# Setup in one unrolled pipeline, routings turned through TensorE, and new operand layouts in a two-layer macaron network

## The chip, the cores and the metric

The kernel runs on one core of one Trainium2 chip. The metric is the time of one execution on the device in microseconds (us). The engines that matter here are TensorE (PE, with its weight loads as PEld), VectorE (DVE), ScalarE (ACT), GpSimd (POOL) and SyncE (SP), which issues the DMAs.

## The reference

The input x is 2 sequences of 512 tokens with 512 features each. Two layers are computed on it, and every sublayer sees a layer norm (`ln`) of x:

```
x = x + 0.5 * ffn0(ln(x));  x = x + attn0(ln(x));  x = x + 0.5 * ffn0(ln(x))
x = x + 0.5 * ffn1(ln(x));  x = x + attn1(ln(x));  x = x + 0.5 * ffn1(ln(x))

ffn0: xn = ln(x) * gamma + beta; sig = sign(xn)            # 64 tiles of 8 features, 8 clusters of 8 tiles
      tile = argmax of sig @ tile_sigs.T in the cluster with the largest sig @ cluster_sigs.T
      x_slice = the 8 features of that tile; mn, mx = its min, max over all tokens of the tile
      u = (x_slice - mn) / (mx - mn); spline by bases and slopes at u, added to the 8 features
attn0: q, k, v with biases, rotary; kp, qp = random features (sin, cos) of the unit vectors
      kv = einsum('bhsf,bhsd->bsfd', kp, v); out = einsum('bhsf,bsfd->bhsd', qp, kv) @ Wo.T + bo
      # the sum runs over the heads of one token, so tokens are independent of each other
attn1: causal differential attention, two softmaxes per head pair, o = o1 - lam * o2, rms norm, Wo
ffn1: x = fwht(x * SU_ug); up, gate = x @ W_up.T * Wscale, x @ W_gate.T * Wscale; silu(gate) * up
      x = fwht(x * SU_dp) @ W_down.T * Wscale_dp
```

The second of the two min and max tables depends on x after attn0, so ffn0 is routed twice.

## The kernel before, in words

Tokens lie on the 128 partitions. The 2,048 rows that the kernel holds are 16 token tiles of 128 (`NT`), in 4 chunks of 512 (`NCH`, `TPC` = 4 tiles each). Weights and the large activations are kept as pairs of fp16 numbers, a high part and the rest of it (names end in `_hi` and `_lo`): ACT writes the high part from PSUM and DVE the low part. Each engine has its own hand-written program; counting semaphores (`gate`) order them, and loops over chunks are hardware loops (`Fori`). The stages, by time:

1. **Setup** (`setup_sync` L480, `setup_pool` L544, `setup_tensor` L570, `setup_scalar` L629, `setup_vector` L686). PE turns three groups of layer-0 weights (L566). Then a loop of 4 iterations follows, each with two groups of W_up and W_gate: a group of 4 tiles is scaled by row on DVE (L720), turned on PE (L566), split into high and low parts by ACT (L653) and DVE (L726), multiplied by a Hadamard matrix on PE (L597, 32 matmuls of 512 columns) and split again (ACT L659, DVE L735). Each iteration also holds the first routing of one chunk: layer norm statistics (`token_stats_vector` L337: DVE L343 to L362, ACT L371 to L376), gamma and beta on POOL (L539, L541), the sign on ACT (L384) and everything else on DVE (`routing_choice` L403 and `routing_ends` L427: products and sums over 128x2048 elements). POOL mixes one of four row blocks of W_down in each iteration (L556, L558). A stage behind the loop turns, splits and multiplies W_down (PE L614, L624, L625; DVE L763, L771) and stores it to HBM.
2. **b loop** (`b_tensor` L1031 and its siblings): layer-0 attention of a chunk, with the second routing of the chunk before (`last`) and the spline and norm of the next one (`next`) inside. Rotary and features take the projections in 6 steps `z`. SP spreads the features with 36 DMAs (L1191). The attention proper takes 32 groups of 16 tokens in 16 pairs `y`: PE makes the scores of a pair (L1082, 2 matmuls of 256 columns), DVE masks them (L1260), and PE multiplies by the values (L1093, 16 matmuls of 64 columns on four column tiles).
3. **First ffn1** (L1012 products with the turned weights).
4. **c loop** (`c_tensor` L1529 and its siblings): differential attention. A step `t` takes two heads and one block of 128 keys. Its exponentials come from ACT (L1681), DVE casts them to fp16 (L1788), and the low parts are taken on DVE for head 0 (L1790) and on POOL for head 1 (L1738). PE then multiplies by the values (L1616 to L1626).
5. **Second ffn1.**

The low parts in the c loop are ordered by these lines:

```
# PE, c_tensor
gate(pe, s["c_p_lo0"], nth(i, 1, STEPS, t + 1), s["gates"])
gate(pe, s["c_p_lo1"], nth(i, 1, STEPS, t + 1), s["gates"])
# ACT, c_scalar, ahead of the exponentials of step t
if t >= 2:
    gate(e, s["c_p_lo0"], nth(i, 1, STEPS, t - 1), s["gates"])
    gate(e, s["c_p_lo1"], nth(i, 1, STEPS, t - 1), s["gates"])
```

## Time and profile before

| | us |
|---|---|
| median of 3 runs | 2706.0 (2699.02 to 2713.09) |
| the profiled execution | 2700.26 |
| its span, first to last instruction | 2697.7 |
| PE busy | 2077.6 (77%) |
| DVE busy | 1280.5 (47%) |
| ACT busy | 720.1 (27%) |
| POOL busy | 390.0 (14%) |

The profile is of one execution. Its span is 2.6 us shorter than its time on the device. The shares are averages over stages with different limits, so they say little about a change that touches three of the five stages; the table by stage further down does. A matmul group is busy from its first start to its last modelled end, so a busy PE can still be slow. The granted clock of TensorE (PEclk) has two levels here, 1.0 for 2.4 GHz and 0.5 for 1.2 GHz; a mean between them is a mixture in time.

### The profile page before, as it was taken

The page shows a single profiled execution, that of the slowest core. Times are in us where ns is not written, and L with a number is a line of the kernel's source. Part 1 is how long each engine was busy: PE and PEld are TensorE (multiplying, and loading weights), DVE is VectorE, ACT ScalarE, POOL GpSimd, SP SyncE. Part 2 cuts the span into 40 slices and gives each one's busy share as a digit, 9 for nine tenths or more (in the row PEclk, how much of TensorE's full clock was granted, in tenths as well). Part 3 has the DMA queues.
Part 4 walks back from the last instruction along what each step waited for, and adds up shares of the span by engine and source line. Part 5 has one row for each costly group of instructions (what it writes and reads, how often), then busy time and mean ns, then how long its engine had stood idle before and what let it go on. Part 6 is the DMA issues. An engine that isn't in the chain of part 4 may idle for free.

```text
span 2697.7 us, 33465 instructions
## 1 busy us (share of the span) xinstructions
PE 2077.6 (77%) x11495; PEld 935.6 (35%) x11495; DVE 1280.5 (47%) x2219; ACT 720.1 (27%) x1102; POOL 390.0 (14%) x268
## 2 busy tenths in 40 slices
PE   4343386756567619999999888787879789999998
PEld 2121232213122204444444333333334334444443
DVE  3887746555656474242412167464756622121221
ACT  2332222131221312221212135243342522121210
POOL 0666010200102000000000024132332400000000
PEclk8676675757658559999999988988979899999999
DMA  7000311010000110000000000000000010000000
GB/s 257 31 31 0 69 21 31 16 35 16 18 17 16 36 63 1 1 0 0 0 32 0 32 1 2 2 1 2 1 1 1 1 63 1 16 0 16 0 16 16
DMA packets 74133, 58.09 MB, mean 22 GB/s; under 512 B 49185, under 2 KB 60705, under 8 KB 72993
## 3 DMA queue, kind: packets, MB, share of 16 engines
q1 hardware_dynamic: 74016, 56.57, 7.3%
q8 instruction: 69, 1.13, 0.2%
q14 instruction: 48, 0.39, 0.0%
HBM read 36.63 MB, written 10.49 MB: 17 GB/s over the span
## 4 chain that ended last, share of the span: by engine, by line
PE 58%; DVE 22%; issue 7%; ACT 5%; SPq 2%; POOL 2%; DMA 1%; DVEq 1%; ACTq 0%; POOLq 0%
PE ps L1012 46%; DVE arena L1788 2%; PE ps L1082 2%; SPq L1191 2%; PE ps L1093 1%; DVE arena L435 1%; DVE arena L720 1%; DVE arena L431 1%; PE ps L1635 1%; PE ps L1597 1%; PE ps L799 1%; POOL arena L1743 1%; PE ps L1550 1%; DVE arena L343 1%; DVE arena L411 1%
## 5 line engine op out<-in xcount | busy, mean ns | idle before, releaser
L1012 PE MATMUL ps<-arena 128*128 128x512 f16 (+1 forms) x6048 | 1344.4, 383 | 60.9 <-DVE arena L1810 16.2
L1012 PEld LDWEIGHTS ps<-arena 128*128 128x128 f16 x6048 | 593.0, 99 | 787.9 <-issue 112.5
L1363 DVE SCALAR_TENSOR_TENSOR arena<-ps,arena 128x512 f32<-128x512 f32 x128 | 88.5, 692 | 441.4 <-PE ps L1012 433.9
L1337 ACT ACTIVATE arena<-ps 128x512 f32<-128x512 f32 x128 | 76.6, 598 | 529.4 <-PE ps L1012 522.0
L597 PE MATMUL ps<-arena 128*128 128x512 f16 x256 | 72.6, 453 | 127.9 <-DVE arena L726 127.9
L1392 DVE SCALAR_TENSOR_TENSOR arena<-ps,arena 128x512 f32 (+1 forms) x32 | 22.1, 691 | 307.3 <-PE ps L1012 307.3
L1738 POOL TENSOR_TENSOR arena<-arena 128x512 f16<-128x512 f32 (+3 forms) x128 | 132.9, 1038 | 223.5 <-DVE arena L1788 223.5
L1732 POOL TENSOR_TENSOR arena<-arena 128x512 f16<-128x512 f32 x32 | 37.0, 1157 | 859.8 <-ACT arena L1660 859.8
L1759 DVE TENSOR_REDUCE arena<-ps 128x2 f32<-128x256 f32 (+3 forms) x128 | 98.7, 818 | 62.8 <-PE ps L1550 60.7
L1788 DVE CAST arena<-arena 128x1024 f16<-128x1024 f32 (+3 forms) x128 | 93.5, 730 | 72.9 <-PE ps L1626 43.0
L1681 ACT ACTIVATE arena<-ps 128x1024 f32<-128x1024 f32 (+3 forms) x128 | 89.5, 701 | 91.8 <-POOL arena L1738 41.7
L1082 PE MATMUL ps<-arena 96*128 96x256 f16 x128 | 64.8, 600 | 55.8 <-DMA arena<-arena 33.7
L1170 POOL TENSOR_TENSOR arena<-arena 128x512 f32<-128x512 f32 x24 | 32.3, 1347 | 438.3 <-ACT arena L1126 438.3
L1367 DVE TENSOR_TENSOR arena<-arena 128x512 f16<-128x512 f32 x128 | 87.2, 682 | 2.0 <-ACT arena L1341 1.8
L597 PEld LDWEIGHTS ps<-arena 128*128 128x128 f16 x256 | 28.0, 112 | 170.5 <-issue 151.2
L1341 ACT ACTIVATE arena<-arena 128x512 f16<-128x512 f32 x128 | 79.6, 622 | 19.9 <-DVE arena L1363 19.9
L1597 PE MATMUL ps<-arena 32*128 32x512 f16 (+3 forms) x768 | 81.5, 320 | 0.0
L1260 DVE TENSOR_TENSOR arena<-ps,arena 128x256 f32<-128x256 f32 x128 | 48.4, 420 | 65.9 <-PE ps L1082 65.1
L1790 DVE TENSOR_TENSOR arena<-arena 128x512 f16<-128x512 f32 (+3 forms) x128 | 71.8, 561 | 15.2
L1337 ACT ACT_TABLE_LOAD x12 | 15.4, 1283 | 191.2 <-PE ps L1012 191.2
L990 PE MATMUL ps<-arena 128*128 128x128 f32 x80 | 19.5, 425 | 60.4 <-ACT arena L971 42.8
L1056 PE MATMUL ps<-arena 128*24 128x512 f32 x48 | 32.9, 777 | 34.4 <-POOL arena L1174 34.2
(235 smaller groups left out, 2473.4 us busy)
## 6 DMA issues: line engine op xcount, KB each, us to landing
arena<-arena SPq DMA_DIRECT2D x144, 64.0 KB, 2.0
arena<-_attn_hidden_states_dram SPq DMA_DIRECT2D x4, 1024.0 KB, 10.5
arena<-in_L_ffn_W_up_dram SPq DMA_DIRECT2D x8, 512.0 KB, 8.3
arena<-in_L_ffn_W_down_dram SPq DMA_DIRECT2D x4, 1024.0 KB, 14.7
arena<-in_L_ffn_W_gate_dram SPq DMA_DIRECT2D x8, 512.0 KB, 4.2
...
```

The lines of the kernel that those rows point to most:

```text
L597: ins = pe.matmul(k.ps[:, 4 + kc, :], sign, part[:, jc, :], start=(n == 0), stop=(n == 7))
L1012: ins = pe.matmul(out, left[a](c), right[b](c), start=(at == 0), stop=(at == 3 * n - 1))
L1082: ins = pe.matmul(k.ps[:, 4 + y % 2, 256 * q:256 * q + 256].rearrange("p (t h) -> p t h", h=16), k.ksg[0:96, 2 * y + q, :], k.qs[0:96, :, ...
L1337: e.activation(k.silu[:, f % 2, :], k.ps[:, 2 * (f % 2), :], ACT.Silu, scale=1.0 / (W_SCALE * A_SCALE))\
L1341: e.activation(k.act_hi[:, f - 1, :], k.prod[:, (f - 1) % 2, :], ACT.Copy).then_inc(s["f_hi"], 1)
L1363: e.scalar_tensor_tensor(out=k.prod[:, f % 2, :], in0=k.ps[:, 1 + 2 * (f % 2), :], scalar=1.0 / W_SCALE, in1=k.silu[:, f % 2, :], op0=ALU. ...
L1367: e.tensor_tensor(k.act_lo[:, f - 1, :], k.prod[:, (f - 1) % 2, :], k.act_hi[:, f - 1, :], ALU.subtract)\
L1597: pe.matmul(k.ps[:, bank, queries], x[rows, 4 + b, keys], y[rows, b, queries], start=False, stop=False)
L1681: e.activation(k.p32[:, t % 2, :, queries], k.ps[:, 2 * (t % 2):2 * (t % 2) + 2, queries], ACT.Exp, scale=SCORE)\
L1738: e.tensor_tensor(k.p_lo[:, t % 2, 1, queries], k.p32[:, t % 2, 1, queries], k.p_hi[:, t % 2, 1, queries], ALU.subtract).then_inc(s["c_p_l ...
L1759: e.tensor_reduce(k.mx[:, u, 4 * b + 2 * j:4 * b + 2 * j + 2], k.ps[:, bank:bank + 2, 0:(u + 1) * P], AXX, ALU.max).then_inc(s["c_max"], 1)
L1788: e.tensor_copy(k.p_hi[:, t % 2, :, queries], k.p32[:, t % 2, :, queries]).then_inc(s["c_p_hi"], 1)
```

## The change

**Setup.** It becomes one unrolled program. The statistics of all 16 token tiles are taken once, ahead of the 4 iterations. The small vectors (scales, gamma, beta, biases) are loaded as rows into `k.rt` and turned by one PE operation; gamma and beta are no longer spread over the partitions. The row scaling of W_up and W_gate (L720) is gone, and the scale is applied in ffn1 instead, where ACT and DVE take it in place of a constant. Each iteration has three groups now: two of W_up or W_gate, and one W_down block, which had its own stage. The turned tiles have 2 PSUM banks and the multiplied ones 2, where each had 4. The stores of W_down lie between the loads of later groups on SP. The loads of two biases, `bv` and `bo`, come behind the last routing.

**Routings.** Both use PE. The normed rows are turned (L416 of the new file); ACT applies gamma and beta and takes the sign, features now on the partitions. Fp16 matmuls with a matrix of signs make 64 keys for each token (L427, L429), DVE takes the maximum and the one-hot row, PE turns that (L438) and spreads it into a mask (L449), DVE multiplies 4 blocks of 512 by it (L497), and 16 fp32 matmuls with 8 columns each cut out the slice (L459).

**Attention of the b loop.** The scores lie heads first instead of tokens first. The score matmul's moving operand is read in runs of 16 fp16 numbers where each number was 1,024 bytes from the one before. The matmul with the values now reads fp32 numbers that are 64 bytes apart where it read runs of 16. The copy that prepares the keys, the mask and the load of the values (8 DMAs for 1) follow the new layout.

**c loop.** DVE takes the low parts of both heads in one operation, and POOL's L1738 is gone.

```diff
+def route_turn_tensor(k, pe, i, n, c, banks):
+
+    s = k.s
+    if c == 0:
+        gate(pe, s["z_scaled"], i + n, s["gates"])
+    if c < 2:
+        gate(pe, s["r_picked"], nth(i, n, KC, 2), s["gates"])
+    else:
+        gate(pe, s["r_y"], nth(i, n, KC, c - 1), s["gates"])
+    for u in range(TPC):
+        ins = pe.transpose(k.ps[:, banks[c % 2], u * P:(u + 1) * P], k.y[:, u, c * P:(c + 1) * P], k.c["ident"])
+    ins.then_inc(s["r_turned"], 1)
+
+
+def route_key_tensor(k, pe, i, n, bank):
+
+    s = k.s
+    gate(pe, s["r_sign"], nth(i, n, KC, KC), s["gates"])
+    gate(pe, s["r_cut"], i + n, s["gates"])
+    for u in range(TPC):
+        out = k.ps[:, bank, u * NTILE:(u + 1) * NTILE]
+        pe.matmul(out, k.one16, k.key16, start=True, stop=False)
+        for c in range(KC):
+            ins = pe.matmul(out, k.sgt[:, c, u * P:(u + 1) * P], k.tsig[:, c, :], start=False, stop=(c == KC - 1))
+    ins.then_inc(s["r_key"], 1)
+
+
+def route_hot_tensor(k, pe, i, n, bank):
+
+    s = k.s
+    gate(pe, s["r_hot"], i + n, s["gates"])
+    for u in range(TPC):
+        ins = pe.matmul(k.ps[0:NTILE, bank, u * P:(u + 1) * P], k.onehot[:, bass.ds(i * TPC + u, 1), :].squeeze(1),
+                        k.ident16, start=True, stop=True)
+    ins.then_inc(s["r_hot_turned"], 1)
+
+
+def route_mask_tensor(k, pe, i, n, c, banks):
+
+    s = k.s
+    gate(pe, s["r_oht"], i + n, s["gates"])
+    if c >= 2:
+        gate(pe, s["r_picked"], nth(i, n, KC, 2 + c - 1), s["gates"])
+    pe.matmul(k.ps[:, banks[c % 2], :], k.expand[:, c * P:(c + 1) * P], k.hot_t, start=True, stop=True)\
+        .then_inc(s["r_mask"], 1)
+
+
+def route_slice_tensor(k, pe, i, n, bank):
+
+    s = k.s
+    gate(pe, s["r_picked"], nth(i, n, KC, 2 + KC), s["gates"])
+    for u in range(TPC):
+        for c in range(KC):
+            ins = pe.matmul(k.ps[:, bank, 256 + u * DSL:256 + (u + 1) * DSL], k.y[:, u, c * P:(c + 1) * P], k.c["lane"],
+                            start=(c == 0), stop=(c == KC - 1))
+    ins.then_inc(s["r_slice"], 1)
...
+def route_sign_scalar(k, e, i, n, c, banks):
+
+    s = k.s
+    gate(e, s["r_turned"], nth(i, n, KC, c + 1), s["gates"])
+    y = feature_block(k.y, c)
+    e.activation(y, token_columns(k.ps[:, banks[c % 2], :]), ACT.Identity, bias=k.beta[:, c:c + 1],
+                 scale=k.gamma[:, c:c + 1]).then_inc(s["r_y"], 1)
+    gate(e, s["r_y"], nth(i, n, KC, c + 1), s["gates"])
+    e.activation(token_columns(k.sgt[:, c, :]), y, ACT.Sign).then_inc(s["r_sign"], 1)
...
+    gate(e, s["r_key"], i + n, s["gates"])
+    key = k.ps[:, bank, 0:TPC * NTILE].rearrange("p (u t) -> p u t", u=TPC)
+    V.link(e.tensor_reduce(k.kmax, key, AXX, ALU.max))
+    e.tensor_tensor(k.onehot[:, bass.ds(i * TPC, TPC), :], key, bcast(k.kmax.unsqueeze(2), [P, TPC, NTILE]),
+                    ALU.is_equal).then_inc(s["r_hot"], 1)
...
+    gate(e, s["r_mask"], nth(i, n, KC, c + 1), s["gates"])
+    y = feature_block(k.y, c)
+    e.tensor_tensor(y, token_columns(k.ps[:, banks[c % 2], :]), y, ALU.mult).then_inc(s["r_picked"], 1)
...
+    e.tensor_scalar(k.off, hot, 1.0, BIG, ALU.subtract, ALU.mult)
+    gate(e, s["r_slice"], i + n, s["gates"])
+    cells = k.ps[:, bank, 256:256 + TPC * DSL].rearrange("p (u j) -> p u j", u=TPC)
+    e.tensor_reduce(k.ends[:, :, 0], cells, AXX, ALU.max)
+    V.link(e.tensor_reduce(k.ends[:, :, 1], cells, AXX, ALU.min))
+    e.tensor_copy(k.sliced[:, bass.ds(i * TPC, TPC), :], cells).then_inc(s["r_cut"], 1)
     V.link(e.tensor_scalar(k.ends[:, :, 1], k.ends[:, :, 1], -1.0, None, ALU.mult))
...
+    wide = [P, TPC, 2, NTILE]
+    V.link(e.tensor_tensor(k.cand, bcast(k.off.unsqueeze(2), wide), bcast(k.ends.unsqueeze(3), wide), ALU.add))
+    V.link(e.tensor_reduce(k.best, k.cand.rearrange("p u a t -> p a t u"), AXX, ALU.max))
+    e.tensor_tensor(k.acc, k.acc, k.best, ALU.max).then_inc(s["routed"], 1)
+    gate(e, s["routed"], i + n, s["gates"])
...
+    pe.wait_ge(s["ss_set"], 1)
+    for i in range(NCH):
+        turned(i, 0)
+        mixed(i, 0, range(KC))
+        for c in range(KC):
+            route_turn_tensor(k, pe, i, 1, c, ROUTE_BANK)
+        turned(i, 1)
+        route_key_tensor(k, pe, i, 1, KEY_BANK)
+        mixed(i, 1, range(KC))
+        route_hot_tensor(k, pe, i, 1, ROUTE_BANK[0])
+        turned(i, 2)
+        for c in range(KC):
+            route_mask_tensor(k, pe, i, 1, c, ROUTE_BANK)
+        mixed(i, 2, (0, 1))
+        route_slice_tensor(k, pe, i, 1, KEY_BANK)
+        mixed(i, 2, (2, 3))
...
-    with pe.Fori(0, UG_GROUPS // 2) as i:
-        group(i, 0)
-        group(i, 1)
...
+        if g >= 3 and g % 2:
+            store_down(g // 2 - 1)
...
+    store_down(3)
+    sp.wait_ge(s["routed"], NCH)
     sp.dma_start(k.bv, d["L0_attn_bv"].partition_broadcast(P)).then_inc(s["b_in"], 16)
...
+    first(0)
+    setup_stats_vector(k, V)
+    setup_scale_vector(k, V)
+    first(1)
+    setup_norm_vector(k, V)
+    first(2)
+    for i in range(NCH):
+        turned(i, 0)
+        mixed(i, 0, range(KC))
+        turned(i, 1)
+        route_choice_vector(k, V, i, 1, KEY_BANK)
+        mixed(i, 1, range(KC))
+        turned(i, 2)
+        for c in range(KC):
+            route_pick_vector(k, V, i, 1, c, ROUTE_BANK)
+        mixed(i, 2, (0, 1))
+        mixed(i, 2, (2, 3))
+        route_ends_vector(k, V, i, 1, KEY_BANK)
...
+        if last is not None:
+            m = 1 + NCH
+            if z == 2:
+                gate(pe, s["b_v_in"], nth(i, 1, TPC, TPC + 2), s["gates"])
+            if z in (2, 3):
+                route_turn_tensor(k, pe, last, m, 2 * z - 4, SECOND_BANK)
+                route_turn_tensor(k, pe, last, m, 2 * z - 3, SECOND_BANK)
+            if z == 4:
+                route_key_tensor(k, pe, last, m, SECOND_KEY)
+            if z == 5:
+                route_hot_tensor(k, pe, last, m, SECOND_BANK[0])
+            if z >= 6:
+                route_mask_tensor(k, pe, last, m, 2 * z - 12, SECOND_BANK)
+                route_mask_tensor(k, pe, last, m, 2 * z - 11, SECOND_BANK)
...
+        if z == 4 and last is not None:
+            route_slice_tensor(k, pe, last, 1 + NCH, SECOND_KEY)
+            gate(pe, s["r_cut"], last + 2 + NCH, s["gates"])
...
-                ins = pe.matmul(k.ps[:, 4 + y % 2, 256 * q:256 * q + 256].rearrange("p (t h) -> p t h", h=16),
-                                k.ksg[0:96, 2 * y + q, :], k.qs[0:96, :, toks].rearrange("p h t -> p t h"),
-                                start=True, stop=True)
+                ins = pe.matmul(k.ps[:, 4 + y % 2, 256 * q:256 * q + 256].rearrange("p (h t) -> p h t", h=16),
+                                k.ksg[0:96, 2 * y + q, :], k.qs[0:96, :, toks], start=True, stop=True)
...
-                                    k.sm[:, (y - 1) % 2, q].rearrange("p (a j) h -> p j a h", j=4)[:, j],
+                                    k.sm[:, (y - 1) % 2, q].rearrange("p h (a j) -> p j a h", j=4)[:, j],
...
-            routing_choice(k, V, last, 1 + NCH, "")
+            route_choice_vector(k, V, last, 1 + NCH, SECOND_KEY)
...
-        routing_ends(k, V, last, 1 + NCH, "")
+        for c in range(KC):
+            route_pick_vector(k, V, last, 1 + NCH, c, SECOND_BANK)
+        route_ends_vector(k, V, last, 1 + NCH, SECOND_KEY)
...
-            e.activation(k.silu[:, f % 2, :], k.ps[:, 2 * (f % 2), :], ACT.Silu, scale=1.0 / (W_SCALE * A_SCALE))\
+            e.activation(k.silu[:, f % 2, :], k.ps[:, 2 * (f % 2), :], ACT.Silu, scale=k.wscale[:, FB + f:FB + f + 1])\
...
-        if t < STEPS:
-            queries = slice(t % TPC * P, CH)
-            gate(e, s["c_p_hi"], nth(i, 1, STEPS, t + 1), s["gates"])
-            e.tensor_tensor(k.p_lo[:, t % 2, 1, queries], k.p32[:, t % 2, 1, queries], k.p_hi[:, t % 2, 1, queries],
-                            ALU.subtract).then_inc(s["c_p_lo1"], 1)
...
-            e.tensor_tensor(k.p_lo[:, t % 2, 0, queries], k.p32[:, t % 2, 0, queries], k.p_hi[:, t % 2, 0, queries],
-                            ALU.subtract).then_inc(s["c_p_lo0"], 1)
+            e.tensor_tensor(k.p_lo[:, t % 2, :, queries], k.p32[:, t % 2, :, queries], k.p_hi[:, t % 2, :, queries],
+                            ALU.subtract).then_inc(s["c_p_lo"], 1)
```

On DVE, in one iteration of the setup loop. The names are lines and operations, `arena` is SBUF and `ps` is PSUM. Before, from the low parts of the first group to the masked rows (L726 low parts of turned tiles, L735 of multiplied ones, L408 to L424 the choice of the tile, L431 and L435 the slice):

```order
L735 SCALAR_TENSOR_TENSOR arena<-ps,arena 128x512 x4
L726 SCALAR_TENSOR_TENSOR arena<-ps,arena 128x4x128 x4
L408 TENSOR_TENSOR arena<-arena 128x2048
L411 TENSOR_REDUCE arena<-arena 128x256
L412 TENSOR_REDUCE arena<-arena 128x32
L414 SCALAR_TENSOR_TENSOR arena<-arena 128x256
L417 SCALAR_TENSOR_TENSOR arena<-arena 128x64 x4
L422 TENSOR_REDUCE arena<-arena 128x4
L424 TENSOR_TENSOR arena<-arena 128x256
L735 SCALAR_TENSOR_TENSOR arena<-ps,arena 128x512 x4
L431 TENSOR_TENSOR arena<-arena 128x2048
L435 TENSOR_REDUCE arena<-arena 128x32
```

After, the same place (L901 low parts of turned tiles, L910 and L916 of multiplied ones, L487 and L488 the choice, L497 the masked rows, L508 to L510 the slice from PSUM):

```order
L910 SCALAR_TENSOR_TENSOR arena<-ps,arena 128x512 x4
L901 SCALAR_TENSOR_TENSOR arena<-ps,arena 128x4x128 x4
L487 TENSOR_REDUCE arena<-ps 128x4
L488 TENSOR_TENSOR arena<-ps,arena 128x256
L910 SCALAR_TENSOR_TENSOR arena<-ps,arena 128x512 x4
L901 SCALAR_TENSOR_TENSOR arena<-ps,arena 128x512 x4
L497 TENSOR_TENSOR arena<-ps,arena 128x4x128 x4
L916 SCALAR_TENSOR_TENSOR arena<-ps,arena 128x512 x4
L505 TENSOR_SCALAR arena<-arena 128x256
L508 TENSOR_REDUCE arena<-ps 128x4
L509 TENSOR_REDUCE arena<-ps 128x4
L510 COPY arena<-ps 128x32
```

The seven operations of the choice have become two, the product and the reduction over 2,048 elements have become four products of 512, and the W_down group (the second L901 and L916) stands in the iteration.

On SP, at the end of setup (L524 and L634 load the random matrix, L531 and L623 store W_down). Before:

```order
L524 DMA arena<-in_L_attn_rand_matrix_dram 32x16x1 x8
L526 DMA arena<-in_L_attn_bv_dram 128x256
L527 DMA arena<-in_L_attn_bo_dram 128x512
L531 DMA wd_hi_dram<-arena 2048x1x128
L531 DMA wd_lo_dram<-arena 2048x1x128
```

After:

```order
L634 DMA arena<-in_L_attn_rand_matrix_dram 32x16x1 x8
L623 DMA wd_hi_dram<-arena 2048x1x128
L623 DMA wd_lo_dram<-arena 2048x1x128
L638 DMA arena<-in_L_attn_bv_dram 128x256
L639 DMA arena<-in_L_attn_bo_dram 128x512
```

The two biases have moved behind the last store and the last routing. PE and DVE wait for them, as before, ahead of the first spline.

On PE, in an iteration of the b loop, between the last norm sums (L1056, L1219) and the angles of the features (L1066, L1246), where L1063 and L1243 are the six projections. Before:

```order
L1056 MATMUL ps<-arena 24x512 x2
L1063 MATMUL ps<-arena 128x512 x5
...
L1063 MATMUL ps<-arena 128x512
L1066 MATMUL ps<-arena 128x512 x6
```

After:

```order
L449 MATMUL ps<-arena 128x512 x2
L1219 MATMUL ps<-arena 24x512
...
L449 MATMUL ps<-arena 128x512 x2
L1243 MATMUL ps<-arena 128x512 x4
...
L459 MATMUL ps<-arena 128x8 x16
...
L1243 MATMUL ps<-arena 128x512
...
L1243 MATMUL ps<-arena 128x512
L1246 MATMUL ps<-arena 128x512 x6
```

The mask and the slice of the second routing now stand in front of two of the projections.

## Rows read from the trace of the kernel before

**Rows 1.** Windows, whole kernel: stretch, busy of each engine (instructions), PEclk, DMA share, GB/s.

```profile
39.00:279.00 240.00, 90.08 (x400) 45.74 (x400) 183.06 (x248) 76.44 (x108) 130.50 (x40) 0.68 0.12 42
279.00:312.00 33.00, 18.92 (x186) 17.49 (x187) 23.10 (x40) 15.65 (x29) 0.00 (x0) 0.81 0.66 130
...
1380.00:2160.00 780.00, 658.29 (x4639) 289.78 (x4637) 404.95 (x620) 270.31 (x423) 189.74 (x176) 0.91 0.01 4
2160.00:2698.00 538.00, 516.57 (x2399) 235.35 (x2397) 121.51 (x223) 103.80 (x173) 0.00 (x0) 0.99 0.04 16
```

**Rows 2.** Timeline, third setup iteration: start, length, engine, line, operation, [idle before <-releaser].

```profile
170.20 2.28 DVE L720 TENSOR_TENSOR arena<-arena 128x2048 f32<-128x2048 f32 x1
170.67 8.99 PE L597 MATMUL ps<-arena 128*128 128x512 f16 x32 [27.01 <-DVE arena L726]
...
179.50 1.91 PE L566 MATMUL ps<-arena 128*128 128x128 f32 x16
...
182.75 2.93 ACT L376 ACTIVATE arena<-arena 128x512 f32 x4 [2.92 <-DVE arena L362]
...
187.87 2.06 ACT L653 ACTIVATE arena<-ps 128x512 f16<-128x512 f32 x4
189.26 2.47 DVE L726 SCALAR_TENSOR_TENSOR arena<-ps,arena 128x512 f16<-128x512 f32 x4
...
217.93 3.83 DVE L435 TENSOR_REDUCE arena<-arena 128x2048 f32 x1 [0.26 <-DVE arena L431]
...
229.19 2.28 DVE L720 TENSOR_TENSOR arena<-arena 128x2048 f32<-128x2048 f32 x1
```

**Rows 3.** Timeline, end of setup and first spline.

```profile
305.51 0.38 PE L460 MATMUL ps<-arena 128*64 128x128 f32 x2
...
309.48 0.60 PE L790 MATMUL ps<-arena 128*64 128x128 f32 x4 [3.59 <-DVE arena L858]
```

**Rows 4.** DMA issues: tensor, queue, count, KB each, us from issue to landing.

```profile
arena<-in_L_attn_bo_dram SPq DMA_DIRECT2D x1, 256.0 KB, 5.7
```

**Rows 5.** Timeline, attention of the second chunk.

```profile
590.20 1.02 PE L1082 MATMUL ps<-arena 96*128 96x256 f16 x2
591.15 0.65 PE L1093 MATMUL ps<-arena 128*32 128x64 f32 x16
...
591.74 1.02 PE L1082 MATMUL ps<-arena 96*128 96x256 f16 x2
...
593.03 0.76 DVE L1260 TENSOR_TENSOR arena<-ps,arena 128x256 f32<-128x256 f32 x2 [0.78 <-PE ps L1082]
```

**Rows 6.** Windows, the same attention.

```profile
589.00:612.00 23.00, 22.49 (x269) 8.06 (x268) 13.18 (x34) 1.79 (x3) 0.00 (x0) 0.50 0.00 0
```

**Rows 7.** Chain of waits, second routing in the b loop: start, length, what.

```profile
527.52 2.29 DVE arena L431
...
540.44 3.35 DVE arena L326
```

**Rows 8.** Timeline, c loop, from step 4 of one chunk.

```profile
1775.22 1.02 ACT L1681 ACTIVATE arena<-ps 128x1024 f32<-128x1024 f32 x1 [1.71 <-POOL arena L1738]
...
1777.34 0.69 DVE L1790 TENSOR_TENSOR arena<-arena 128x512 f16<-128x512 f32 x1
1777.37 1.61 POOL L1738 TENSOR_TENSOR arena<-arena 128x512 f16<-128x512 f32 x1 [2.16 <-DVE arena L1788]
...
1777.95 1.45 DVE L1788 CAST arena<-arena 128x768 f16<-128x768 f32 x1
...
1782.95 1.02 ACT L1681 ACTIVATE arena<-ps 128x1024 f32<-128x1024 f32 x1 [1.63 <-DVE arena L1790]
...
1799.28 0.54 DVE L1788 CAST arena<-arena 128x768 f16<-128x768 f32 x1
```

**Rows 9.** Waits, c loop (1380 to 2160): who <- whom: us in total, times, longest.

```profile
ACT arena L1681 <- POOL arena L1738: 41.7, 29, 2.1
...
PE ps L1624 <- POOL arena L1738: 14.8, 27, 0.9
```

596 lines of the change are left out of this document (309 added, 287 removed).

## The prediction

> **What bounds the kernel now.** I read the windows first, since the change touches stages with different limits. In the last ffn1 phase the second column (PE busy) nearly fills the first (the stretch): 516.57 of 538 us [rows 1]. There, and in the first such phase with the same code, the new scale operands change only what ACT and DVE do beside a saturated PE, and I cost them at nothing. The loop of setup is the opposite: 240 us with PE busy for 90.08 and DVE for 183.06, at a PEclk of 0.68 [rows 1]. Then I read one iteration in the timeline. Row scaling L720 starts at 170.20 and again at 229.19, so an iteration takes 59.0 us, and the brackets say why: PE's L597 stood idle for 27.01 us behind DVE's L726, and DVE was then in the choice and the slice of the routing, up to 3.83 us for one operation (L435) [rows 2]. So setup is bound by one long chain through DVE.
>
> In the attention of the b loop the timeline shows a period of 1.54 us for one pair of groups (590.20 to 591.74): 0.95 us from the start of the two L1082 to that of L1093, and 0.59 us for L1093 [rows 5]. PE is busy for 22.49 of 23 us there, at a clock of 0.50, and DVE for 13.18 [rows 6]. PE bounds that stretch. The two L1082 have 512 columns, so one costs 0.95 / 512 = 1.86 ns. At 1.2 GHz a column lasts 0.83 ns, and L597, whose 32 matmuls of 512 contiguous columns took 8.99 us, costs 0.55 ns a column at mixed clocks [rows 2]. The strided read is the natural reason for the factor of 2.2.
>
> In the c loop ACT's exponentials wait for POOL's low parts 41.7 us in total, and PE for the same 14.8 us [rows 9]; the timeline shows how POOL's 1.61 us operation also stretches the cast that runs beside it on DVE: 1.45 us for 768 columns, and 0.54 us for the same form without it [rows 8].
>
> **Setup.** New iteration, built from the old rows. The three groups of turned tiles: a tile is 1.91/4 = 0.48 us on PE (L566), 2.06/4 = 0.52 on ACT (L653) and 2.47/4 = 0.62 on DVE (L726) [rows 2]. With 2 banks, two tiles are in flight, so a group takes two rounds of 1.6 us and their hand-overs, at most four; I take 5.6 us. Three of them are 16.8. Two groups of L597 at 9.0 are 18.0. The W_down group has 8 matmuls of 512 instead of 32, and is then paced by ACT and DVE at some 1 us a block: 4.0. Signs: 8 ACT operations of 512 at 2.93/4 = 0.73 us (L376) are 5.9. Picks: 4 DVE operations at the 0.69 us of L1790 [rows 8] with a little for the PSUM read: 3.0. The slice: 16 fp32 matmuls; the nearest row is L566 with 0.12 us each, 1.9 us, double at the lower clock; 2.9. The ends: eight small operations stood between the end of L435 and L726 before, in 229.19 - 221.76 - 2.47 = 4.96 us; there are seven now, narrower, and I take 3.6. Hand-overs between engines, 8 of about 0.3 (0.26 ahead of L435 [rows 2]): 2.4. Sum 56.6 us. Part of this overlaps (signs beside the next turned group), part is longer at the lower clock; bounds 52 and 62.
>
> Four iterations are 226 us against 236. The old ones started at about 279 - 236 = 43 us. The new ones start some 4 us later, because the statistics of all 16 tiles stand ahead, so they end at 273. What is gained is the separate W_down stage behind the loop: its last product was followed by L460 at 305.51, and the first spline began at 309.48 [rows 3]. The new one begins behind the loads of the biases, which now start behind the last routing: 273 + 1 + 5.7 us landing [rows 4] = 280. Before, that load was under the W_down stage and cost nothing. With 1 us of small work the spline begins at 281: **28 us** gained. At 52 us an iteration it is 46, at 62 it is 6.
>
> **Attention of the b loop.** With one run of 16 numbers the score matmuls should reach the clock: 512 columns at 0.83 ns are 0.43 us instead of 0.95. L1093 keeps its 0.59 if its new stride costs nothing. Then PE needs 1.02 us a pair. DVE's part is 0.76 us for the masks, with 0.78 us of idle time before them [rows 5], so it isn't the bound until 0.76 plus the output's low parts. I take 1.16 us, 0.38 less than 1.54, in 16 pairs and 4 chunks: **24 us**.
> The PV read is the doubtful part. L1093 reads 64 fp32 columns for each of 16 matmuls, 1,024 in 0.59 us, by four column tiles side by side. No row shows such a read with a stride. The nearest row is L1082, 1.86 ns a number when each lies alone. If the four tiles read side by side, each has 256 numbers, 0.48 us, below 0.59: no cost. If they share the read, it is 1024 x 1.86 = 1.9 us.
> The Trainium skill ("SBUF — State Buffer", section "Door 1: The DMA port swizzle") says that SBUF has lines of 16 bytes and that an access needs two hits in a line to run at full rate. The slow L1082 agrees. By the same rule, the new read of L1093, one number per line, loses what L1082 gains. The page doesn't say what this costs with several column tiles; that is the first rival.
>
> **Second routing in the b loop.** On the path stood, behind the last rotary step, the tail from L431 at 527.52 to the reciprocal L326 at 540.44, 12.9 us [rows 7]. Now there stand four picks (3.0), the slice behind four of the projections, 512 fp32 columns each at about 1 us (4.1, partly beside the picks), 1.9 to 3.9 us for the slice, and ends of 3.6: 11 to 13 us and the norm behind them. PE gets some 10 us more work in the steps z, and DVE loses more than that. I take **0**, with -4 to +4 us for each of 3 chunks: 12 us either way. The eight loads of the values are issued before they are needed, under the SP queue's spread; they cost nothing unless that cover goes.
>
> **c loop.** From one 1,024-wide exponential to the next, 1775.22 to 1782.95, four steps take 7.73 us [rows 8]. DVE pays for both heads now: the low part is 1.38 us (2 x 0.69) instead of 0.69, 2.0 more over four steps of falling width. It gets back the stretched casts: 1.45 to 0.54 for one, and some 0.9 for the two narrower ones together, 1.8 in all. DVE's sum stays equal. But the low parts of head 1 end with DVE's and not 1.61 us after the cast plus a hand-over, so the waits of ACT and PE for POOL go, 56.5 us in total [rows 9]; part of it comes back as a wait for DVE, which is nearly full in such a unit. I take 0.6 us of 7.73, in 32 units: **20 us**, bounds 0 and 36.
> The skill's page (section "Who interferes with whom") says that a VectorE operation with two SBUF inputs competes with GpSimd's reads. [...]
>
> **Sum.** 28 + 24 + 0 + 20 = 72 us. Against the profiled execution, 2700.3 - 72 = 2628; it ran 5.7 us under the median of 2706.0, from which the same sum gives 2634. I predict 2635.
>
> **Rivals.**
> 1. *The strided PV read is shared by the column tiles.* A pair then costs 0.43 + 1.9 = 2.33 us, or up to 2.75 with weight loads that don't hide: +0.8 to +1.2 us in 64 pairs, +51 to +77 us instead of -24. With the rest kept: 2706 - 48 + 51 to 77 = 2709 to 2735; I put it at 2725, slower. It decides the sign from a pair of about 2.5 us on. For it speaks that the old reads, if four neighbours came with each at 1.86 ns, would take 256 x 1.86 = 0.48 us, close to the 0.59 measured; against it that four tiles have their own streams. Chance 0.14.
> 2. *The score matmul isn't bound by its read.* Nothing gained there: 2706 - 48 = 2658. Against it: no other reason for 2.2 times the column time at 0.50. Chance 0.10.
> 3. *Setup's chain is as long as before.* Each iteration passes from PE to ACT to DVE and back some 12 times, two banks give little slack, and the clock stays low: 62 us, 6 gained, 2657. Chance 0.17.
> 4. *c loop bound by DVE at once.* Its equal sum on DVE gives nothing: 2655. Chance 0.12.
> 5. *The chains shorten more:* 52 us an iteration and 36 in the c loop, 2600. Chance 0.12.
> The forecast holds 0.35.
>
> **How the numbers follow.** Less than 0.5% (13.5 us) is about what a measurement of this kernel can tell from no change. All but rival 1 are faster unless two of them fall together: 0.86 - 0.03 = 0.83, plus nothing from rival 1. Rivals 2, 3 and 4 together give 2706 - 6 = 2700, which I count with the lower end of rival 1 as the same: 0.07. Slower 0.10. The range reaches from rival 5 to rivals 3 and 4 with 30 us for two at once: 2590 to 2690.
>
> **What would show it.** Setup: the loop's W_up groups follow each other every 56 us, the first spline starts near 281, and its last wait is for the bias load. Attention: a pair every 1.16 us, two score matmuls in 0.43 us, the value matmuls still at 0.59. c loop: four steps in 7.1 us, exponentials waiting for DVE and no longer for POOL, the 768-wide cast at 0.54. Wrong would be: value matmuls above 1.1 us per 16 (rival 1), PE idle for DVE for more than 10 us at a stretch in setup (rival 3), a c loop unit of 7.7 us (rival 4).

## The result, and the profile after

The changed kernel takes 2624.27 us (median of 4 runs, 2620.0 to 2629.41) against 2705.55 us before: the ratio is 0.9699, with a 95% interval of 0.9668 to 0.9731. That is 81 us less; 72 were forecast. The page of the changed kernel shows POOL busy for 7% of the span where it was for 14%, and PE a little busier (busy time, share of the span, instructions), and then TensorE's granted clock in 40 slices:

```profile
PE 2128.3 (81%) x12014; PEld 1000.6 (38%) x12014; DVE 1123.6 (43%) x2118; ACT 742.2 (28%) x1152; POOL 179.6 (7%) x132
...
PEclk8777668678686779999999898998989899999999
```

The windows of the changed kernel (stretch, busy of PE, PEld, DVE, ACT and POOL, PEclk, DMA share, GB/s), with setup up to its last routing first and the last ffn1 phase second:

```profile
41.00:259.00 218.00, 168.30 (x786) 98.73 (x786) 90.99 (x152) 98.08 (x151) 74.40 (x32) 0.75 0.17 49
...
2080.00:2618.00 538.00, 516.70 (x2399) 235.19 (x2397) 125.37 (x223) 109.59 (x173) 0.00 (x0) 0.99 0.04 16
```

In setup PE is busy for 168.30 of 218 us, where it was for 90.08 of 240, and DVE for 90.99 where it was for 183.06 [rows 1]. PE's busy time in the last phase is the same to 0.2 us (516.57 before). Where the time went, in us, by marks that both traces have (the first PE operation of the first spline, then the first value projection of each chunk of the b loop, then the residual sums at the chunk ends of the c loop; "the table's turn" is PE turning the table of minima and maxima):

| stretch | before | after | gained |
|---|---|---|---|
| setup to the first spline | 309.48 | 267.47 | 42.0 |
| first spline to first chunk | 33.4 | 33.8 | -0.4 |
| chunk 1 of the b loop | 133.3 | 123.3 | 10.0 |
| chunk 2 | 169.4 | 163.5 | 5.9 |
| chunk 3 | 164.7 | 160.1 | 4.6 |
| chunk 4 and the last routing alone, to the table's turn (L460, L554) | 173.7 | 168.9 | 4.8 |
| from there, through the first ffn1, to the end of the first c chunk (1705.2, 1634.2) | 721.2 | 717.2 | 4.0 |
| three more c chunks | 461.5 | 452.4 | 9.1 |
| rest | 531.0 | 531.6 | -0.6 |

Setup gave 42, the b loop 25, and the last three rows 12.5. Of these, the first can't be told from nothing. From the table's turn to the last residual sum of the first c chunk it was 728.9 us before, and over the eleven traces that have the new code there (this one and ten of the experiments) it is between 722.0 and 732.2. The three c chunks behind it are steadier, 439 to 448 us in those eleven traces (444.4 here) and 454 to 458 in the three that have the old code.

Inside the b loop the four stretches from the start of the attention (L1082, L1262) to the next mark went from 236.4 us in total to 208.0, 28.4 less. The four stretches ahead of the attention went from 404.7 to 407.7, 3.0 more: -1.4, 0.0, +1.4 and +3.0 by chunk. The timeline of PE in one setup iteration of the changed kernel, where [rows 2] showed the old one (L712 is the product that was L597, L459 the slice):

```profile
155.83 9.09 PE L712 MATMUL ps<-arena 128*128 128x512 f16 x32 [1.42 <-DVE arena L901]
...
175.23 9.63 PE L712 MATMUL ps<-arena 128*128 128x512 f16 x32
...
193.47 6.83 PE L459 MATMUL ps<-arena 128*128 128x8 f32 x32
...
207.22 1.71 PE L669 MATMUL ps<-arena 128*128 128x128 f32 x8 [3.49 <-DVE arena L901]
210.34 9.14 PE L712 MATMUL ps<-arena 128*128 128x512 f16 x32 [1.42 <-DVE arena L901]
...
258.60 0.61 PE L554 MATMUL ps<-arena 128*64 128x128 f32 x2 [4.56 <-DVE arena L515]
267.47 1.03 PE L952 MATMUL ps<-arena 128*64 128x128 f32 x4 [8.26 <-DVE arena L1020]
```

An iteration takes 54.5 us from 155.83 to 210.34 (54.3 on the mean of three), and PE never waits for longer than 3.5 us in it. The slice takes 6.7 us until PE goes on, at a granted clock of 0.50. The last two rows are the table's turn and the first spline, 8.9 us apart where they were 4.0 [rows 3]: the bias loads.

The attention of the second chunk, first at the lower clock and then at the higher one (L1262 the scores, L1272 the values, L1445 the masks):

```profile
538.20 0.61 PE L1262 MATMUL ps<-arena 96*128 96x256 f16 x2
...
538.74 0.67 PE L1272 MATMUL ps<-arena 128*32 128x64 f32 x16
...
539.34 0.61 PE L1262 MATMUL ps<-arena 96*128 96x256 f16 x2
...
546.00 1.65 DVE L1445 TENSOR_TENSOR arena<-ps,arena 128x256 f32<-128x256 f32 x4 [0.50 <-PE ps L1262]
...
546.24 0.39 PE L1262 MATMUL ps<-arena 96*128 96x256 f16 x2
...
547.05 0.65 PE L1272 MATMUL ps<-arena 128*32 128x64 f32 x16 [0.42 <-DVE arena L1445]
```

the window of its second half:

```profile
543.00:553.00 10.00, 8.59 (x171) 4.57 (x164) 8.39 (x22) 1.19 (x2) 0.00 (x0) 1.00 0.01 2
```

and one pair of the first chunk:

```profile
388.81 0.39 PE L1262 MATMUL ps<-arena 96*128 96x256 f16 x2
389.13 0.64 PE L1272 MATMUL ps<-arena 128*32 128x64 f32 x16
389.70 0.39 PE L1262 MATMUL ps<-arena 96*128 96x256 f16 x2
```

At the lower clock a pair takes 1.14 us (538.20 to 539.34) and up to 1.37, against 1.54 [rows 5]. Some 5 us after the pairs begin the clock rises to 1.00, where it was 0.50 throughout [rows 6]. The scores then last 0.39 us, and some pairs take only 0.90, with PE going from one operation to the next without a wait (388.81 to 389.70). Others take 1.23 to 1.39 us, since PE waits for the masks (0.42 us at 547.05) while DVE is busy for 8.39 of 10 us. At the higher clock the mean is 1.10 us in the second and third chunk and 0.98 in the first and fourth. So PE is still the bound in some pairs, and DVE in the others.

The c loop, four steps from one 1,024-wide exponential to the next:

```profile
1705.76 1.02 ACT L1864 ACTIVATE arena<-ps 128x1024 f32<-128x1024 f32 x1 [1.73 <-PE ps L1784]
...
1707.88 1.23 DVE L1968 TENSOR_TENSOR arena<-arena 128x1024 f16<-128x1024 f32 x1
...
1709.03 0.55 DVE L1966 CAST arena<-arena 128x768 f16<-128x768 f32 x1
...
1709.23 0.60 ACT L1864 ACTIVATE arena<-ps 128x512 f32<-128x512 f32 x1 [1.02 <-DVE arena L1968]
...
1712.75 1.02 ACT L1864 ACTIVATE arena<-ps 128x1024 f32<-128x1024 f32 x1 [1.41 <-PE ps L1784]
```

It is 6.99 us where it was 7.73 [rows 8], the 768-wide cast is 0.55 instead of 1.45, and the 512-wide exponential waits for DVE's low parts. In the whole c loop the exponentials wait for DVE's low parts for 26.7 us, where they waited 41.7 for POOL's and 10.3 for DVE's.

### The profile page after: what moved, and what is told of

It reads as the page before. It is cut to its first block, busy times and chain, and to the rows that moved or that the text cites. A ratio compares the mean times of both kernels' runs of the same rounds, so it can differ in the third digit from the quotient of the medians.

```text
span 2618.2 us, 33051 instructions
## 1 busy us (share of the span) xinstructions
PE 2128.3 (81%) x12014; PEld 1000.6 (38%) x12014; DVE 1123.6 (43%) x2118; ACT 742.2 (28%) x1152; POOL 179.6 (7%) x132
## 4 chain that ended last, share of the span: by engine, by line
PE 67%; DVE 16%; issue 7%; ACT 6%; SPq 1%; DMA 1%; POOL 1%; DVEq 1%; ACTq 0%; POOLq 0%
PE ps L1174 48%; PE ps L712 3%; PE ps L459 2%; DVE arena L1966 1%; PE ps L1782 1%; PE ps L961 1%; PE ps L1272 1%; PE ps L1819 1%; PE ps L1243 1%; SPq L1376 1%; DVE arena L1445 1%; PE ps L1735 1%; PE ps L669 1%; PE ps L1219 1%; PE ps L1214 1%
## 5 line engine op out<-in xcount | busy, mean ns | idle before, releaser
L1174 PEld LDWEIGHTS ps<-arena 128*128 128x128 f16 x6048 | 592.8, 99 | 776.3 <-issue 95.7
L1548 DVE SCALAR_TENSOR_TENSOR arena<-ps,arena 128x512 f32<-128x512 f32 x128 | 96.2, 751 | 434.1 <-PE ps L1174 426.6
L1522 ACT ACTIVATE arena<-ps,arena 128x512 f32<-128x512 f32 x128 | 88.2, 689 | 518.7 <-PE ps L1174 518.5
L1968 DVE TENSOR_TENSOR arena<-arena 128x1024 f16<-128x1024 f32 (+3 forms) x128 | 113.0, 883 | 15.2
L1966 DVE CAST arena<-arena 128x1024 f16<-128x1024 f32 (+3 forms) x128 | 64.4, 503 | 65.5 <-PE ps L1810 37.8
L1526 ACT ACTIVATE arena<-arena 128x512 f16<-128x512 f32 x128 | 79.5, 621 | 19.9 <-DVE arena L1548 19.9
L669 PE MATMUL ps<-arena 128*128 128x128 f32 x240 | 43.4, 336 | 47.4 <-DVE arena L901 27.5
L712 PE MATMUL ps<-arena 128*128 128x512 f16 x256 | 72.4, 452 | 5.7 <-DVE arena L901 5.7
L1262 PE MATMUL ps<-arena 96*128 96x256 f16 x128 | 29.0, 321 | 54.7 <-issue 32.4
L1152 PE MATMUL ps<-arena 128*128 128x128 f32 x80 | 18.7, 410 | 67.1 <-ACT arena L1133 47.8
L1445 DVE TENSOR_TENSOR arena<-ps,arena 128x256 f32<-128x256 f32 x128 | 47.4, 419 | 38.6 <-PE ps L1262 36.7
L1353 POOL TENSOR_TENSOR arena<-arena 128x512 f32<-128x512 f32 x24 | 26.2, 1090 | 466.5 <-ACT arena L1303 466.5
L1243 PE MATMUL ps<-arena 128*128 128x512 f32 x48 | 33.1, 827 | 27.7 <-DVEq L1418 25.0
L1841 ACT ACTIVATE arena<-ps 128x512 f32<-128x512 f32 x32 | 19.1, 597 | 128.3 <-PE ps L1174 128.3
```

What stands on the lines that cost most here:

```text
L712: ins = pe.matmul(k.ps[:, bank, :], sign, part[:, jc, :], start=(n == 0), stop=(n == 7))
L1174: ins = pe.matmul(out, left[a](c), right[b](c), start=(at == 0), stop=(at == 3 * n - 1))
L1445: ins = e.tensor_tensor(k.sm[:, y % 2, q], k.ps[:, 4 + y % 2, 256 * q:256 * q + 256] .rearrange("p (h t) -> p h t", h=16), bcast(k.c["same ...
L1522: e.activation(k.silu[:, f % 2, :], k.ps[:, 2 * (f % 2), :], ACT.Silu, scale=k.wscale[:, FB + f:FB + f + 1])\
L1526: e.activation(k.act_hi[:, f - 1, :], k.prod[:, (f - 1) % 2, :], ACT.Copy).then_inc(s["f_hi"], 1)
L1548: e.scalar_tensor_tensor(out=k.prod[:, f % 2, :], in0=k.ps[:, 1 + 2 * (f % 2), :], scalar=k.wscale[:, f:f + 1], in1=k.silu[:, f % 2, :], o ...
```

## Experiments

Times are medians; each ratio is to the kernel before on the same chip, with its 95% interval. The changed kernel stands at 2624.3 us and 0.9699. The experiments ran on three chips, and an interval is 5 to 12 us wide to either side, so differences of some 10 us are read from the traces, stage by stage. A letter says which theory of the expectation a run bears out.

**1. POOL back in the c loop.**

```diff
-            e.tensor_tensor(k.p_lo[:, t % 2, :, queries], ...).then_inc(s["c_p_lo"], 1)       # DVE
+            e.tensor_tensor(k.p_lo[:, t % 2, 0, queries], ...).then_inc(s["c_p_lo0"], 1)      # DVE
+            e.tensor_tensor(k.p_lo[:, t % 2, 1, queries], ...).then_inc(s["c_p_lo1"], 1)      # POOL
```

> The changed kernel with the c loop as it was: POOL takes the low part of the second head again, DVE that of the first. Theory A: the hand-over to POOL and the casts that POOL slows are all of what the c loop gained. The loop gets back its 13 us: 2624 + 13 = 2637 us, the first four-step unit goes from 7.0 back to 7.7 us, and a 768-wide cast beside POOL takes 1.45 us again. Theory B: the c loop gained because the stage starts in another state (buffers moved, other clock). Then 2624 us and units of 7.0 us stay.

2633.6 us (0.9735, 0.9695 to 0.9775), 9 us more. Exponentials wait for POOL 36.9 us again, 19 of the 32 casts of 768 columns take 1.36 to 1.45 us again, and the three last c chunks take 457.7 us instead of 444.4. Theory A; its 13 us are the 13.3 of these chunks, and they lie within the interval of the whole.

**2. Tokens first in the attention of the b loop.**

```diff
-                                k.ksg[0:96, 2 * y + q, :], k.qs[0:96, :, toks], start=True, stop=True)
+                                k.ksg[0:96, 2 * y + q, :], k.qs[0:96, :, toks].rearrange("p h t -> p t h"),
+                                start=True, stop=True)
...
```

The value matmul, the mask, the keys and the load of the values go back with it.

> The changed kernel with the attention of the b loop as it was: tokens first in scores, masks and keys, one load of the values. Theory A: the strided read of the score matmuls is all of it. A pair costs 1.54 us again, the clock there falls to 0.50, and the time is 2624 + 64 x 0.42 = 2651 us. Theory B: part of the 25 us that the b loop gained comes from the routing on PE (POOL and DVE freed in the steps z). Then the time is only some 2635 to 2640 us, and the steps z keep a gain.

2653.0 us (0.9811, 0.9771 to 0.985), 29 us more. The window of one attention with this layout, and two scores and values in the timeline:

```profile
553.00:573.00 20.00, 18.15 (x230) 6.74 (x230) 11.26 (x28) 2.39 (x4) 0.00 (x0) 0.50 0.01 2
```

```profile
551.95 1.02 PE L1262 MATMUL ps<-arena 96*128 96x256 f16 x2
552.90 0.65 PE L1273 MATMUL ps<-arena 128*32 128x64 f32 x16
553.49 1.02 PE L1262 MATMUL ps<-arena 96*128 96x256 f16 x2
```

1.54 us again, at 0.50. The four stretches from the attention on take 236.0 us, as before the change (236.4), and those ahead of it 408.2, as in the changed kernel (407.7). So all of the b loop's gain hangs on this layout, and the routing's move to PE gained nothing there. Theory A.

**3. Value matmuls with runs of 16 again.**

```diff
-                                    k.sm[:, (y - 1) % 2, q].rearrange("p h (a j) -> p j a h", j=4)[:, j],
+                                    k.sm[:, (y - 1) % 2, q].rearrange("p (a j) h -> p j a h", j=4)[:, j],
...
-            ins = e.tensor_tensor(k.sm[:, y % 2, q], k.ps[:, 4 + y % 2, 256 * q:256 * q + 256]
+            ins = e.tensor_tensor(k.sm[:, y % 2, q].rearrange("p t h -> p h t"), k.ps[:, 4 + y % 2, 256 * q:256 * q + 256]
```

> Scores stay heads first, but the mask is written tokens first (DVE writes 64 bytes apart), so the value matmuls read runs of 16 again. Theory A: the four column tiles read side by side and their stride costs nothing: 16 value matmuls stay at 0.58 us, a pair at 1.1 us, 2624 us. Theory B: the stride costs something that now hides under DVE: value matmuls fall below 0.5 us per 16, with the pair still 1.1 us since DVE bounds it, 2624 us. If the strided write slows DVE's masks (0.38 us for one now), a pair gets longer by twice that.

2642.3 us (0.9779, 0.9737 to 0.982). Its timeline:

```profile
548.15 0.66 PE L1272 MATMUL ps<-arena 128*32 128x64 f32 x16
548.48 2.15 DVE L1445 TENSOR_TENSOR arena<-ps,arena 128x256 f32<-128x256 f32 x4
...
548.74 0.61 PE L1262 MATMUL ps<-arena 96*128 96x256 f16 x2
...
549.64 0.66 PE L1272 MATMUL ps<-arena 128*32 128x64 f32 x16 [0.30 <-DVE arena L1445]
```

Sixteen value matmuls last 0.66 us with a contiguous read and 0.65 to 0.69 with numbers 64 bytes apart: the stride costs PE nothing (theory A for the read), and rival 1 is out. The same stride on DVE's output does cost: four masks take 2.15 us instead of 1.65, 0.25 us for a pair. A pair doesn't get longer by that much everywhere. At the lower clock the first five pairs of the first chunk take 1.13 to 1.18 us against 1.14, the first four of the second 1.13, 1.49, 1.14 and 1.64 against 1.14, 1.25, 1.16 and 1.34. And the clock stays at 0.50 for the whole attention of all four chunks, though PE is as busy in 10 us as it was at 1.00:

```profile
545.00:555.00 10.00, 8.55 (x128) 3.93 (x126) 8.42 (x17) 1.20 (x2) 0.00 (x0) 0.50 0.02 4
```

Why it stays isn't shown. The starts of the scores spread over 17.8, 20.1, 19.9 and 17.8 us in the four chunks, against 15.3, 17.2, 17.1 and 15.3: 11 us more, from the masks and the lower clock together. The profiled execution is 18.0 us longer; 6.9 of these lie between the b loop and the end of the first c chunk, which this edit doesn't touch. So the whole doesn't price the stride.

**4. Ends behind the next turned group.**

```diff
     for i in range(NCH):
         turned(i, 0)
+        if i:
+            route_ends_vector(k, V, i - 1, 1, KEY_BANK)
...
-        route_ends_vector(k, V, i, 1, KEY_BANK)
+    route_ends_vector(k, V, NCH - 1, 1, KEY_BANK)
```

> In setup, DVE's last small operations of a routing (ends) come behind the low parts of the next iteration's first turned group instead of ahead of them. Theory A: setup is a chain through DVE, and these 3.5 us stand on it in three iterations: 2624 - 10 = 2614 us, iterations of 50.9 instead of 54.3 us. Theory B: the wait goes to ACT or to the multiplied group behind it, since DVE's work is only moved: 2624 us and iterations of 54 us.

2609.0 us (0.966, 0.9615 to 0.9705). Iterations start at 98.33, 149.18 and 200.21 us, 50.9 apart, and the table is turned at 250.60 instead of 258.60. An iteration lost 3.4 us, and the first spline starts 8.1 earlier (259.34), which is 8 of the 15 us; the rest is within the interval. Theory A, which had 10 us: the small operations stood on the chain.

**5. Biases loaded early** (`bv` and `bo` moved into memory that the last W_gate group leaves, the loads ahead of the last store and without the wait for `routed`).

> The two bias tensors lie in memory that the last W_gate group leaves, so their loads start before the last routing instead of behind it. Theory A: the first spline waits for them alone: 258.6 to 267.5 us in the changed kernel, against 4.0 us for the same stretch before. 2624 - 5 = 2619 us. Theory B: the stretch is DVE's and the copies', the load is only the last of several: 2624 us.

2615.0 us (0.968, 0.966 to 0.9699), 9 us less. Its timeline shows the wait gone, 2.8 us where 8.9 were, and the first spline starts 7.4 us earlier. Theory A:

```profile
257.26 0.61 PE L554 MATMUL ps<-arena 128*64 128x128 f32 x2 [4.55 <-DVE arena L515]
260.07 1.03 PE L952 MATMUL ps<-arena 128*64 128x128 f32 x4 [2.21 <-DVE arena L1020]
```

**6. The slice with the small matrix as weights.**

```diff
-            ins = pe.matmul(k.ps[:, bank, 256 + u * DSL:256 + (u + 1) * DSL], k.y[:, u, c * P:(c + 1) * P], k.c["lane"], ...)
+        ins = pe.matmul(token_columns(k.ps[0:DSL, bank, :]), k.c["lane"], feature_block(k.y, c), ...)
```

> In setup and in the last routing the slice is made with the 8-column matrix as the weights and the masked rows as 4 moving operands of 512, then a copy on DVE and 4 small turns, instead of 16 matmuls with a full fp32 weight load each for 8 columns. Theory A: these 6.6 us of PE stand on the chain; 3.5 us remain: 4 x 3 in setup and 3 in the last routing, 2624 - 15 = 2609 us. Theory B: PE has slack there (the multiplied W_down blocks wait for ACT and DVE anyway) and the copy on DVE is one more hand-over: 2620 to 2628 us.

2621.8 us (0.9704, 0.9683 to 0.9725): nothing. That is theory B's time. Its reason, slack on PE, isn't shown; the trace has another:

```profile
83.76 5.83 PE L470 MATMUL ps<-arena 128*8 128x512 f32 x8 [0.79 <-DVE arena L525]
...
89.62 0.68 DVE L489 COPY arena<-ps 8x512 f32<-8x512 f32 x1 [5.92 <-PE ps L470]
```

Four fp32 matmuls of 512 columns, recorded as 8, take 5.83 us at this clock (0.61 on the mean), and DVE's copy and four small turns follow, where the 16 small matmuls took 6.7. I had sized the new form at 3.5 us.

**7. Signs between the blocks.**

```diff
         mixed(i, 0)
-        for c in range(KC):
-            route_sign_scalar(k, e, i, 1, c, ROUTE_BANK)
         turned(i, 1)
+        for c in range(KC):
+            route_sign_scalar(k, e, i, 1, c, ROUTE_BANK)
+            mixed(i, 1, (c,))
...
```

On PE the second group is turned ahead of the routing's turns and the key comes behind that group; the choice on DVE moves with it.

> In setup the second group is turned ahead of the routing's turns, and ACT takes the 8 sign operations in pairs between the multiplied blocks of that group, where PE is busy with the next block, instead of in one piece of 5.5 us. The key stands behind that group. Theory A: setup is one chain, and the 5.5 us on ACT leave it in each of 4 iterations: 2624 - 20 = 2604 us. Theory B: a block takes PE 2.2 us and ACT then needs 2.0, so ACT becomes late for the blocks, and key, choice and one-hot row get onto the chain behind the group: less than 8 us gained, 2616 us or more.

2610.3 us (0.9657, 0.9629 to 0.9685). The table is turned at 243.69 us, 15 earlier, so an iteration lost 3.7 us of the 5.5 that the signs take. The 14 us of the whole agree. That is halfway between A (20) and B (less than 8).

**8, 9. Experiments 4 to 7 together, and the same without the slice of experiment 6.**

> The changed kernel with the later ends, the early biases, the slice by rows and the signs between the blocks together. Theory A: the pieces stand one behind the other on one chain, so their gains add: 15 (measured) + 5 + 15 + 20 = 55, 2570 us. Theory B: where one chain is shortened another (ACT with its three groups of splits, signs and W_down scaling, some 35 us an iteration, or PE at 33 us) takes over: an iteration can't fall below about 42 us, and half of the sum is what comes, 2595 us.

> The changed kernel with the later ends, the early biases and the signs between the blocks, and with the slice as it is. Theory A: the slice by rows costs PE 5.8 us against 6.8 and a copy more on DVE, so it gives nothing with the others either: 2580 us. Theory B: with the chain shortened elsewhere PE decides, and the form with less PE time is the better one: 2585 us or more here.

With the slice by rows 2580.2 us (0.9558, 0.9538 to 0.9579), without it 2578.7 (0.9526, 0.9486 to 0.9566). The first lies between its theories (2570 and 2595), since the slice's 15 us of theory A didn't come; the second is theory A. The slice form makes no difference again. The three alone gave 15 + 9 + 14 = 38 us, together they gave 46; by the start of the first spline it was 8.1 + 7.4 + 14.9 = 30 us, and 40 together (227.80). So each gain is there in full, as on one chain, and some 10 us come on top. The granted clock of this setup is higher than in the changed kernel (0.75) and with the signs alone (0.77):

```profile
41.00:225.00 184.00, 149.96 (x785) 94.48 (x786) 90.56 (x152) 97.08 (x151) 74.61 (x32) 0.82 0.21 60
```

That fits, but no run separates the clock from the order.

**10. One mask for a pair**, on top of 9.

```diff
-        for q in range(2):
-            ins = e.tensor_tensor(k.sm[:, y % 2, q], k.ps[:, 4 + y % 2, 256 * q:256 * q + 256]
+        ins = e.tensor_tensor(k.sm[:, y % 2].rearrange("p q h t -> p (q h) t"), k.ps[:, 4 + y % 2, :]
...
```

> The last one with the two masks of a pair as one DVE operation of 512 instead of two of 256. Theory A: a pair is now bound by DVE (masks of 0.76 to 0.83 us and a quarter of a low part of 0.68), and one operation of 512 costs 0.69: 0.1 us less in each of 64 pairs, 6 us, 2574 us. Theory B: the two masks let PE start the scores of the next pair earlier, or PE at 1.0 us a pair is the bound at the lower clock: no change, 2580 us.

2572.3 us (0.9512, 0.9472 to 0.9552), 6 us less, the number that A has, though the interval doesn't tell it from nothing. A mask pair takes 0.69 us, and PE's longer idle time before the values is 0.18 instead of 0.42.

```profile
351.74 0.69 DVE L1449 TENSOR_TENSOR arena<-ps,arena 128x512 f32<-128x512 f32 x1 [0.21 <-PE ps L1267]
...
353.68 0.66 PE L1277 MATMUL ps<-arena 128*32 128x64 f32 x16 [0.18 <-DVE arena L1449]
```

But the starts of the scores spread over 14.9, 17.1, 17.4 and 15.0 us in the four chunks, against 15.3, 17.1, 17.1 and 15.3 in experiment 9: 0.5 us less in all, not 6. In the third chunk the clock rose later. So the attention's bound isn't the two masks alone, and A isn't shown; the traces speak for B.

**11, 12. Setup without the first routing, before and after.**

> The kernel before, with the first routing left out of setup: no gamma and beta, no signs, no choice of a tile, no slice and no ends (so no token has a tile in the first spline, whose work is done all the same); the statistics stay. Theory A: about 24 us of DVE operations leave each iteration, and they stood on the chain: iterations of 37 us instead of 59, 2706 - 88 = 2618 us. Theory B: the turned and multiplied groups fill the time anyway, since POOL's mixing (23 us) and the groups' own hand-overs remain: iterations above 45 us, 2650 us.

> The changed kernel, with the first routing left out of setup in the same way (no turns, signs, key, choice, mask, slice or ends). Theory A: the new routing stands on the chain with its signs (5.5), key (2), masks (3.5), slice (6.6) and ends (3.4), 21 us: iterations of 33 us instead of 54.3, 2624 - 85 = 2539 us. The move to PE then bought nothing on the path, and the 42 us of setup came from the row scaling, the statistics taken once and the merged W_down. Theory B: it overlaps more than the old one did, and leaving it out gives less than 12 us an iteration, 2576 us or more; then the move to PE is what paid.

Both leave out the first routing, so no token has a tile in the first spline. Before: 2654.2 us (0.9812, 0.977 to 0.9854), 47 less, iterations of 47.2 us (98.81 to 146.14). After: 2547.2 us (0.9422, 0.9381 to 0.9463), 77 less, iterations of about 35 us. The second has theory A's numbers (35 us, forecast 33): the new routing stands on the chain with 19 us an iteration. The first has theory B's, but the trace of that run says that its cover changed. POOL's mixing, which had come behind gamma and beta, now ran beside the statistics:

```profile
154.98 2.35 POOL L557 TENSOR_TENSOR arena<-arena 128x1024 f32 x1
155.19 2.16 DVE L328 SCALAR_TENSOR_TENSOR arena<-arena 128x4 f32<-128x4 f32 x1
...
157.50 0.16 DVE L329 SCALAR_TENSOR_TENSOR arena<-arena 128x4 f32<-128x4 f32 x1
...
157.81 2.15 DVE L353 TENSOR_TENSOR arena<-arena 128x4 f32<-128x4 f32 x1
```

Operations on 128x4 numbers took 2.15 us, each until POOL's ended, and 0.16 us between two of POOL's. L350, L328, L353, L354, and L327 and L328 once more, lost some 11 us this way in that iteration (0.16 or so each without POOL). An estimate from these rows: if all of it stood on the chain, the iteration would have been about 36 us without it, and the old routing's own share about 23. So the run doesn't price the old routing, and whether the move to PE pays by itself stays open: 19 against something between 12 and 23 us an iteration.

## Why the prediction was right

**Setup: right in kind, too small.** 42 us instead of 28. The iteration was 54.3 us instead of 56.6, which is 9 us in four. The first turned group started at 41.4 and not at 47: on PE it waits for the landing of the first W_up load alone, and the statistics, which I had put ahead of it, run on DVE under that load. That is 6 us. The bias load cost 8.9 us against 8 forecast, where only 2.8 are needed. Within the iteration two terms were wrong against each other: the slice takes 6.7 us and not 2.9 (16 matmuls of 8 columns still load 16 fp32 weights of 128 x 128, recorded in 32 passes of 0.2 us), and the three turned groups cost some 14 us without the ends, not 16.8. The signs (5.5 us, forecast 5.9) and the ends (2.9, forecast 3.6) were about right, and experiments 4 and 7 show them on the chain. The slice's 6.7 us are at 0.50; at 1.00, in the b loop (480.19), it took 3.6. Rival 3 is out: PE is never idle for 10 us in the iterations.

**Attention: right, a little too small.** 24 forecast, 28 by its stretches, 29 by taking the layout back. A pair takes 1.14 us and more at the lower clock, forecast 1.16. What the forecast didn't have is the clock. It rose to 1.00 some 5 us into the pairs, where PE had been busy for 6.22 of 7.20 us (535.80 to 543.00). Before, with PE busy for 22.49 of 23 us [rows 6], it had stayed at 0.50, and in experiment 3 it stayed there too. What raises it isn't shown. It brought little, since DVE became the bound in a part of the pairs.
Rival 1 fell with experiment 3. The Trainium skill's two hits in a 16-byte line ("SBUF — State Buffer", section "Door 1: The DMA port swizzle") hold for the score read, 1.86 ns a number before and 1.04 after (0.53 us for the 512 of a pair), both at 0.50, so rival 2 is out as well. They don't show in the value matmuls on four column tiles: 0.59 us for 1,024 numbers, alone in their lines or not. They last 0.58 us at 1.00, so the clock doesn't set them either; what does isn't shown.

**Second routing: right at 0, within its bounds.** From the first value projection of the second chunk to its attention it was 111.2 us (476.17 to 587.39) and is 111.3 (424.54 to 535.80); the third chunk lost 1.4 and the fourth 3.0. The fourth's stretch was 99.7 to 102.9 us over the traces with this code (99.9 before), so 3 us is also its scatter.

**c loop: right in kind, too large.** The last three chunks gained 9 us by the stages and 13 by experiment 1, the whole 9 by experiment 1; forecast 20 with bounds of 0 and 36. The unit read, 7.73 us, became 6.99, even a little better than the 0.6 forecast (the low part of both heads is 1.23 us and not 1.38). The step that failed is the multiplication by 32. Over seven units of a chunk the starts of the wide exponentials went from 68.8, 68.4 and 68.7 us to 65.0, 64.6 and 64.6 in the first three chunks, 0.5 a unit. In the fourth they didn't gain at all:

```profile
2076.31 1.79 ACT L1681 ACTIVATE arena<-ps 128x1024 f32<-128x1024 f32 x2 [2.07 <-PE ps L1599]
...
2134.48 1.01 ACT L1681 ACTIVATE arena<-ps 128x1024 f32<-128x1024 f32 x1
```

```profile
1996.33 1.02 ACT L1864 ACTIVATE arena<-ps 128x1024 f32<-128x1024 f32 x1 [2.07 <-PE ps L1784]
...
2054.80 1.01 ACT L1864 ACTIVATE arena<-ps 128x1024 f32<-128x1024 f32 x1
```

That is 58.2 us before and 58.5 after. Single units say little: in the second chunk one got 2.2 us shorter and two got 0.3 longer. Why the fourth chunk gained nothing no run shows. Rival 4, no gain in the c loop, is out by experiment 1.

**Sum.** 42 - 0.4 + 28.4 - 3.0 + 12.5 = 79.5, the whole difference of the spans (2697.7 and 2618.2), against 72. Setup's 14 and the attention's 4 too little partly cancel with the c loop's 7 and the second routing's 3 too much. That the total came out within 8 us is in that part luck.
